# A GRU and attention layer: VectorE's order around the gates and the first norm, and the PSUM bank of one transpose

## Chip, cores and metric

One core of one Trainium2 chip. The metric is the device time of one execution in microseconds, less being better. The kernel before takes 58.65 us, the median of 3 runs (58.57 to 58.78).

## What is computed

Two graph layers over 512 nodes with 128 features, each with a residual and a layer norm without weights. The first aggregates over edges and applies a GRU cell, the second is graph attention with 4 heads:

```python
agg = jnp.einsum('ij,jh,ijh->ih', adj, node_features, T)
gi = agg @ w_ih.T + b_ih
gh = node_features @ w_hh.T + b_hh
r = sigmoid(ir + hr); z = sigmoid(iz + hz)
nn_ = tanh(in_ + r * hn)
L0 = (1.0 - z) * nn_ + z * node_features
x = _layernorm(x + L0)
...
h = jnp.einsum('ni,hid->hnd', x, W)
energy = leaky_relu(s_src[:, :, None] + s_dst[:, None, :], 0.2)
attention = softmax(where(adj > 0, energy, NEG_INF))
x = _layernorm(x + einsum('hij,hjd->hid', attention, h))
```

The adjacency matrix is sparse (512 by 512, few ones), the edge table has one row of 128 for each pair of nodes.

## The kernel before, in words

The kernel is written for the five engines by hand: each engine has its own program (`@block.tensor`, `@block.vector`, `@block.scalar`, `@block.gpsimd`, `@block.sync`), and the order of the calls in it is the order of the engine's queue. Engines meet through semaphores: `then_inc` at the producer, `wait_ge` at the consumer. Nothing is reordered. A branch on `flag` takes a sparse or a dense path; with this input it is the sparse one, and only its order of calls is spoken of here (the dense path has a loop over both groups that the diff adjusts too).

Nodes lie as 4 tiles of 128. Tiles 0 and 1 are group 0, tiles 2 and 3 are group 1; many steps run once for each group g. Edges lie in 10 chunks of 128, in the order `ORDER`; five belong to each group. The steps around the change, for a group:

- **products** (`product`, line 1156): for each chunk, VectorE multiplies gathered edge rows with gathered source rows. The source rows come from TensorE (`source_rows`, line 603) through a PSUM bank, from which ScalarE copies them (`keep_xr`, line 402). k counts chunks in the order of use, so products 5 to 9 are those of group 1.
- **aggregate** (line 749, TensorE), then ScalarE's copy `keep_agg` (line 482), then TensorE's gate matmuls (`gates`, line 640), ScalarE's three tanh for r, z and the candidate (`gates`, line 437), and between them VectorE's `gated` (line 1078: the candidate before its tanh) and `mixed` (line 1087: three instructions that end in yT, the transposed sum of residual and GRU output).
- **raw_x1** (line 653, TensorE) transposes yT into a PSUM tile `y_ps`. `project` (line 662, TensorE) multiplies yT with the attention weights.
- **moments** (line 1102, VectorE): two bn_stats and two bn_aggr on `y_ps`. The reciprocal deviation comes for group 0 from GpSimd by a power (line 361), for group 1 from ScalarE's square root (`deviation`, line 446) and VectorE's reciprocal (`invert`, line 1096).
- **keep_u, split_u** (lines 1116 and 1162, VectorE): the attention logits' node terms, in three bf16 parts. **scaled_h** (line 457, ScalarE): h. **split_h** (line 1170, VectorE): the middle and the low bf16 part of h, the high one being h's own upper half. TensorE gathers h for each edge in three passes (`gather_h`, line 805): the pass s = 1 needs the middle part (`s_hres`), the pass s = 2 the low part (`s_hlo`).
- **normalise** (line 1123, VectorE): x1 itself, two instructions that read `y_ps`. x1 is only needed for the residual at the end; SP copies it (line 309) once all four tiles are there (`s_x1`).
- GpSimd adds up h (`h_sum`, lines 362 to 368) as soon as ScalarE has written it.

`y_ps` is PSUM bank 3, all four tiles. TensorE may not write into a bank in which VectorE is reading, so the group-1 `raw_x1` waits until x1 of group 0 is done (lines 656 and 657). Bank 2 holds the candidate's input part `in_ps`, its first half for group 0, its second half for group 1, and later the transposed logits and the numerators of tiles 0 and 1.

TensorE's order in the stretch: aggregate(0), gates(0), the source rows of the last groups, raw_x1(0), project(0), aggregate(1), gates(1), high and middle gathers of group 0, edge_logits(0), raw_x1(1), project(1), 28 more gather matmuls of which the last 12 need the low part of h, edge_logits(1), and so on (lines 768 to 829).

Of the kernel before, what the change touches and what calls it, by code (L numbers as in the profile page):

```python
# [10 lines left out]
ALU = mybir.AluOpType  # L11
# [9 lines left out]
NC = 10  # L21
# [6 lines left out]
def build_gnn(nc, x, x_turned, adj, adj_first, adj_turned, edge_table, w_hh, w_ih, w_gat, w_gat_turned, columns, out):  # L28
# [10 lines left out]
    with ExitStack() as ctx:  # L39
# [142 lines left out]
        in_ps = tiles4[2]  # L182
        y_ps = tiles4[3]
        sel_bank = [bank[2], bank[3]]
# [347 lines left out]
        def _(pe):  # L532
# [120 lines left out]
            def raw_x1(g):  # L653
                pe.wait_ge(s_yT, g + 1)
                pe.wait_ge(s_wcc, 1)
                if g == 1:
                    pe.wait_ge(s_x1, 2)
                for t in range(2 * g, 2 * g + 2):
                    mm = nc.tensor.transpose(y_ps[:, t], yT[:, t], ident[:])  # L659
                mm.then_inc(s_yp, 1)  # L660
# [275 lines left out]
        def _(dve):  # L936
# [159 lines left out]
            def invert(k):  # L1096
# [3 lines left out]
                nc.vector.reciprocal(rstd[:, ts], spread[:, ts]).then_inc(s_rstd, 1)  # L1100

            def moments(g, link):
                dve.wait_ge(s_yp, g + 1)
                for t in range(2 * g, 2 * g + 2):
                    ins = nc.vector.bn_stats(st6[:, t, 0], y_ps[:, t])
                link(ins)
                for t in range(2 * g, 2 * g + 2):
                    ins = nc.vector.bn_aggr(mv[:, t], st6[:, t, 0:1])
                if g == 0:
                    link(ins)  # L1110
                    nc.vector.tensor_scalar(epsv[:, 0:2], mv[:, 0:2, 1], 4 * EPS, None, ALU.add).then_inc(s_var, 1)  # L1111
                else:
                    ins.then_inc(s_var, 1)
                    invert(1)

            def keep_u(g):
# [4 lines left out]
                                        rstd[:, ts].unsqueeze(2).broadcast_to([P, 2, 2 * NH]), ALU.mult).then_inc(s_u, 1)  # L1121

            def normalise(g):
                for t in range(2 * g, 2 * g + 2):
                    nc.vector.tensor_scalar(x1[:, t], y_ps[:, t], mv[:, t, 0:1], rstd[:, t:t + 1], ALU.subtract, ALU.mult)\
                        .then_inc(s_x1, 1)

# [26 lines left out]
            with dve.If(sparse == 1):  # L1154
# [14 lines left out]

                def split_h(g):  # L1170

                    ts = slice(2 * g, 2 * g + 2)
                    dve.wait_ge(s_h, g + 1)
                    nc.vector.tensor_tensor(h_parts[:, 1, ts], h_parts[:, 0, ts], h3[:, 0, ts], ALU.subtract).then_inc(s_hres, 1)
                    dve.wait_ge(s_hres, g + 1)
                    nc.vector.tensor_tensor(h_parts[:, 2, ts], h_parts[:, 1, ts], h3[:, 1, ts], ALU.subtract).then_inc(s_hlo, 1)
# [3 lines left out]
                gated(0)  # L1180
                product(5)
                product(6)
                mixed(0, link)
                product(7)
                product(8)
                product(9)
                moments(0, link)
                keep_u(0)
                split_u(0)
                split_h(0)  # L1190
                gated(1)
                normalise(0)
                mixed(1, link)
                moments(1, link)
                keep_u(1)
# [8 lines left out]
                nc.vector.tensor_copy(zs[:], shared.unsqueeze(2).broadcast_to([P, 2, 2, NH])).then_inc(s_zs, 1)  # L1204
                split_h(1)
                dve.wait_ge(s_new, 1)
# [49 lines left out]
            with dve.Else():  # L1256
# [14 lines left out]
                for g in range(2):  # L1271
                    gated(g)
                    mixed(g, link)
                    moments(g, link)
                    keep_u(g)
                    normalise(g)
                dve.wait_ge(s_u, 2)
# [78 lines left out]
```

## Time and profile before

| what | value |
|---|---|
| median of 3 runs | 58.65 us |
| profiled execution, its own time | 58.71 us |
| its span, first to last instruction | 57.0 us |
| TensorE busy | 43.2 us (76%), 550 matmuls |
| VectorE busy | 39.6 us (70%), 155 instructions |
| ScalarE busy | 24.9 us (44%), 60 instructions |
| GpSimd busy | 14.6 us (26%) |
| mean granted TensorE clock | 0.969 |

How to read it: busy time is the time in which an engine had an instruction in work, as a share of the span. A busy engine isn't on the critical chain for that reason alone; the chain of waits, followed back from the last instruction, tells which work ended last at each point. In a timeline a merged row gives the start of the first and the time from there to the end of the last of several equal instructions, and in square brackets the idle time of the engine before it and what ended that. Starts of neighbours on VectorE and ScalarE overlap the end before by up to 0.1 us.

### The profile page before, as it was taken

The numbers are of one execution on the slowest core, as the hardware profiler recorded it, in microseconds if no ns is written. First come the engines' busy times: TensorE is split into PE (matmuls) and PEld (weight loads), VectorE is DVE, ScalarE is ACT, GpSimd is POOL, SyncE is SP. The second block draws the span as 40 slices with busy tenths as digits, with TensorE's granted clock in tenths as the row PEclk, the third lists the DMA queues.
The fourth block names the chain that finished last, engine by engine and source line by source line (L and its number), as shares of the span: only waits on it lengthen the run. The fifth ranks groups of instructions, "written<-read, shape, count | busy, mean of one in ns | idle before, by whom it ended". The sixth has DMA issues, their size and how long they took to land.

```text
span 57.0 us, 1512 instructions
## 1 busy us (share of the span) xinstructions
PE 43.2 (76%) x550; PEld 35.4 (62%) x550; DVE 39.6 (70%) x155; ACT 24.9 (44%) x60; POOL 14.6 (26%) x29
## 2 busy tenths in 40 slices
PE   0599687958799999999998979789769899900000
PEld 0133366758589695688996668687759699900000
DVE  3986989999994084702299369963789479999600
ACT  1904636509997343023944085932940191000520
POOL 1940001756767777400000531000510000000000
PEclk9999999999999999999999999999999999999755
DMA  0699970012113131310000000000024200000033
GB/s 0 182 313 340 384 257 0 6 46 58 46 46 46 46 72 32 66 26 0 0 0 0 0 12 0 0 0 6 0 46 100 50 0 0 12 0 12 0 101 89
DMA packets 3033, 3.41 MB, mean 60 GB/s; under 512 B 560, under 2 KB 2096, under 8 KB 3024
## 3 DMA queue, kind: packets, MB, share of 16 engines
q1 hardware_dynamic: 2288, 2.49, 14.0%
q0 software_dynamic: 320, 0.66, 5.2%
q10 hardware_dynamic: 416, 0.14, 0.9%
q8 instruction: 6, 0.10, 0.7%
q14 instruction: 3, 0.02, 0.1%
HBM read 2.76 MB, written 0.26 MB: 53 GB/s over the span
## 4 chain that ended last, share of the span: by engine, by line
DVE 46%; PE 35%; ACT 7%; issue 6%; DVEq 0%; ACTq 0%
DVE colhot L1003 9%; PE bank L676 6%; PE bank L615 6%; PE bank L759 3%; PE bank L808 3%; PE bank L637 3%; DVE st L1136 2%; DVE x1n L1244 2%; DVE held L987 2%; DVE rowhot L992 2%; DVE zmax L1211 2%; DVE zmax_f L1208 2%; PE bank L659 2%; PE bank L763 2%; ACT out_sb L474 2%
## 5 line engine op out<-in xcount | busy, mean ns | idle before, releaser
L347 POOL DMA_INDIRECT edge<-in_L_gnn_edge_table,eidx x10 | 10.1, 1006 | 9.8 <-DVE eidx L1011 7.4
L615 PE MATMUL bank<-x_parts,colhot 128*128 128x128 bf16 x120 | 8.1, 218 | 0.0
L808 PE MATMUL bank<-h_parts,colhot 128*128 128x128 bf16 x120 | 7.9, 219 | 0.0
L615 PEld LDWEIGHTS bank<-x_parts,colhot 128*128 128x128 f16 x120 | 7.2, 96 | 0.3
L808 PEld LDWEIGHTS bank<-h_parts,colhot 128*128 128x128 f16 x120 | 7.3, 96 | 0.2
L1003 DVE TENSOR_TENSOR colhot<-bank,slot_mid 128x512 f16<-128x512 f32 x8 | 5.4, 684 | 0.2 <-PE bank L583 0.2
L676 PE MATMUL bank<-ones_adj 128*128 128x512 f16 x8 | 3.6, 631 | 2.0 <-DVE ones_adj L953 2.0
L405 ACT COPY xr<-bank 128x512 f32<-128x512 f32 (+1 forms) x6 | 3.3, 548 | 2.4 <-PE bank L624 2.4
L583 PE MATMUL bank<-rowhot,posm 128*128 128x128 f16 (+1 forms) x48 | 3.8, 213 | 0.7 <-DVE rowhot L992 0.4
L455 ACT ACT_TABLE_LOAD x3 | 3.8, 1283 | 0.1
L451 ACT ACTIVATE spread<-mv,eps_col 128x2 f32<-128x2 f32 (+1 forms) x2 | 0.6, 296 | 7.1 <-DVE mv L1141 5.7
L637 PE MATMUL bank<-xT,whhT 128*128 128x128 f32 (+1 forms) x12 | 3.7, 403 | 0.0
L1160 DVE TENSOR_TENSOR eprod<-edge,xr 128x128 f32<-128x128 f32 x10 | 2.4, 288 | 1.8 <-ACT xr L405 1.8
L583 PEld LDWEIGHTS bank<-rowhot,posm 128*128 128x128 f16 x48 | 2.9, 115 | 1.0 <-DVE posm L1028 0.6
L676 PEld LDWEIGHTS bank<-ones_adj 128*128 128x128 f16 x8 | 1.0, 141 | 3.7 <-DVE ones_adj L953 2.0
L593 PE MATMUL bank<-jcol,colhot 128*128 128x1 f16 x40 | 2.1, 164 | 1.4 <-DVE colhot L1003 0.7
L861 PE MATMUL bank<-vals,xr 128*128 128x132 f32 x24 | 2.9, 279 | 0.0
L396 ACT ACTIVATE posm<-bank,tot_in 128x512 f16<-128x512 f32 x3 | 2.1, 687 | 2.0 <-DVE tot_in L982 2.0
L593 PEld LDWEIGHTS bank<-jcol,colhot 128*128 128x128 f16 x40 | 1.7, 96 | 2.0 <-DVE colhot L1003 2.0
L361 POOL TENSOR_TENSOR rstd<-epsv,mhalf 128x2 f32<-128x2 f32 x1 | 0.7, 722 | 8.5 <-DVE epsv L1111 8.5
L484 ACT COPY aggT<-bank 128x256 f32<-128x256 f32 x2 | 0.7, 372 | 4.8 <-PE bank L763 4.8
L861 PEld LDWEIGHTS bank<-vals,xr 128*128 128x128 f32 x24 | 2.8, 190 | 0.0
(181 smaller groups left out, 98.1 us busy)
## 6 DMA issues: line engine op xcount, KB each, us to landing
adj_t<-in_adj_turned SPq DMA_DIRECT2D x3, 256.0 KB, 4.0
adj_i<-in_adj_first SPq DMA_DIRECT2D x1, 256.0 KB, 2.7
x_parts<-in_x SPq DMA_DIRECT2D x1, 256.0 KB, 3.6
xT<-in_x_turned SPq DMA_DIRECT2D x1, 256.0 KB, 4.4
x1n<-x SPq DMA_DIRECT2D x4, 64.0 KB, 2.7
whhT<-in_L_gnn_w_hh SPq DMA_DIRECT2D x1, 192.0 KB, 4.4
wT<-in_L_gnn_w_ih SPq DMA_DIRECT2D x1, 192.0 KB, 4.5
edge<-in_L_gnn_edge_table,eidx POOLq DMA_INDIRECT x10, 2.8
```

What stands on the lines that cost most here:

```text
L347: nc.gpsimd.indirect_dma_start(out=edge[:, c], out_offset=None, in_=edge_table, in_offset=bass.IndirectOffsetOnAxis(ap=eidx[:, c:c + 1], a ...
L405: nc.scalar.copy(xr[:, k].rearrange("p f h -> p (f h)")[:, 0:n], x_bank[k % 2][:, 0:n]).then_inc(s_xgc, 1)
L455: nc.scalar.activation(warm[:, k:k + 1], warm[:, 0:1], func)
L583: mm = nc.tensor.matmul(at, posm[:, t, jb::Q], src, start=True, stop=True)
L593: nc.tensor.matmul(idx_bank[:, c:c + 1], cols_at(jb, c), jcol[:, jb:jb + 1], start=(jb == 0), stop=False)
L615: nc.tensor.matmul(x_bank[k % 2][:, i * P:(i + 1) * P], cols_at(jb, c), x3[:, s, jb], start=(jb == 0 and s == 0), stop=(jb == Q - 1 and s ...
L637: return nc.tensor.matmul(at[:, cols], whhT[:, k], xT[:, ts.start:ts.stop].rearrange("h t p -> h (t p)"), start=(ts.start == 0), stop=(k = ...
L676: nc.tensor.matmul(bank[7], ones_adj[:, 0:P], ones_adj[:], start=True, stop=True)
L808: mm = nc.tensor.matmul(hg_at(c), cols_at(jb, c), h3[:, s, jb], start=(g == 0 and s == 0 and c % 4 == 0 and jb == 0), stop=False, skip_gro ...
L861: return nc.tensor.matmul(num_bank[t // 2][:, t % 2], rT_at(c, t), vals[:, c], start=False, stop=False, skip_group_check=True)
L1003: nc.vector.tensor_tensor(colhot[:, :, slots_of(c)], src.rearrange("p (j s) -> p j s", j=Q), want.unsqueeze(1).broadcast_to([P, Q, P]), AL ...
L1160: nc.vector.tensor_tensor(eprod[:, c], edge[:, c], xg_at(c), ALU.mult).then_inc(s_ep, 1)
```

## The change

In the sparse path's VectorE program, products 5 and 6, which stood between `gated(0)` and `mixed(0)`, now stand behind `mixed(0)` with the other three. `split_h` is cut into `middle_h` and `low_h`. `middle_h(0)` keeps its place ahead of `gated(1)`; `low_h(0)` stands between `mixed(1)` and `moments(1)`. `normalise(0)`, which stood between `gated(1)` and `mixed(1)`, is now inside `moments(1)`, behind the bn_aggr of group 1 and ahead of the reciprocal's wait for ScalarE. For group 1 `middle_h` and `low_h` follow each other as before. The tiles of `y_ps` for group 1 move to the first half of bank 2, and TensorE's wait for x1 of group 0 is gone. No instruction is added or taken out.

```diff
--- before.py
+++ after.py
@@ -180,7 +180,7 @@
         r_ps = tiles4[0]
         z_ps = tiles4[1]
         in_ps = tiles4[2]
-        y_ps = tiles4[3]
+        y_ps = [tiles4[3][:, 0], tiles4[3][:, 1], tiles4[2][:, 0], tiles4[2][:, 1]]
         sel_bank = [bank[2], bank[3]]
         x_bank = [bank[4], bank[5]]
         base_bank = bank[6][:, 0:3]
@@ -653,10 +653,8 @@
             def raw_x1(g):
                 pe.wait_ge(s_yT, g + 1)
                 pe.wait_ge(s_wcc, 1)
-                if g == 1:
-                    pe.wait_ge(s_x1, 2)
                 for t in range(2 * g, 2 * g + 2):
-                    mm = nc.tensor.transpose(y_ps[:, t], yT[:, t], ident[:])
+                    mm = nc.tensor.transpose(y_ps[t], yT[:, t], ident[:])
                 mm.then_inc(s_yp, 1)
 
             def project(g):
@@ -1099,10 +1097,15 @@
                 dve.wait_ge(s_std, k)
                 nc.vector.reciprocal(rstd[:, ts], spread[:, ts]).then_inc(s_rstd, 1)
 
+            def normalise(g):
+                for t in range(2 * g, 2 * g + 2):
+                    nc.vector.tensor_scalar(x1[:, t], y_ps[t], mv[:, t, 0:1], rstd[:, t:t + 1], ALU.subtract, ALU.mult)\
+                        .then_inc(s_x1, 1)
+
             def moments(g, link):
                 dve.wait_ge(s_yp, g + 1)
                 for t in range(2 * g, 2 * g + 2):
-                    ins = nc.vector.bn_stats(st6[:, t, 0], y_ps[:, t])
+                    ins = nc.vector.bn_stats(st6[:, t, 0], y_ps[t])
                 link(ins)
                 for t in range(2 * g, 2 * g + 2):
                     ins = nc.vector.bn_aggr(mv[:, t], st6[:, t, 0:1])
@@ -1111,6 +1114,7 @@
                     nc.vector.tensor_scalar(epsv[:, 0:2], mv[:, 0:2, 1], 4 * EPS, None, ALU.add).then_inc(s_var, 1)
                 else:
                     ins.then_inc(s_var, 1)
+                    normalise(0)
                     invert(1)
 
             def keep_u(g):
@@ -1119,11 +1123,6 @@
                 dve.wait_ge(s_rstd, g + 1)
                 nc.vector.tensor_tensor(u_sb[:, ts], proj_bank[g][:, :, H:H + 2 * NH],
                                         rstd[:, ts].unsqueeze(2).broadcast_to([P, 2, 2 * NH]), ALU.mult).then_inc(s_u, 1)
-
-            def normalise(g):
-                for t in range(2 * g, 2 * g + 2):
-                    nc.vector.tensor_scalar(x1[:, t], y_ps[:, t], mv[:, t, 0:1], rstd[:, t:t + 1], ALU.subtract, ALU.mult)\
-                        .then_inc(s_x1, 1)
 
             def residual(ts, ns):
                 return nc.vector.tensor_tensor(y2[:, ns].rearrange("p n (q d) -> p n q d", q=Q)[:, :, ts],
@@ -1167,30 +1166,31 @@
                     nc.vector.tensor_tensor(u_parts[:, ts, :, 2], u_parts[:, ts, :, 1], u3[:, ts, :, 1], ALU.subtract)\
                         .then_inc(s_u3, 1)
 
-                def split_h(g):
+                def middle_h(g):
 
                     ts = slice(2 * g, 2 * g + 2)
                     dve.wait_ge(s_h, g + 1)
                     nc.vector.tensor_tensor(h_parts[:, 1, ts], h_parts[:, 0, ts], h3[:, 0, ts], ALU.subtract).then_inc(s_hres, 1)
+
+                def low_h(g):
+
+                    ts = slice(2 * g, 2 * g + 2)
                     dve.wait_ge(s_hres, g + 1)
                     nc.vector.tensor_tensor(h_parts[:, 2, ts], h_parts[:, 1, ts], h3[:, 1, ts], ALU.subtract).then_inc(s_hlo, 1)
 
                 for k in range(5):
                     product(k)
                 gated(0)
-                product(5)
-                product(6)
                 mixed(0, link)
-                product(7)
-                product(8)
-                product(9)
+                for k in range(5, NC):
+                    product(k)
                 moments(0, link)
                 keep_u(0)
                 split_u(0)
-                split_h(0)
+                middle_h(0)
                 gated(1)
-                normalise(0)
                 mixed(1, link)
+                low_h(0)
                 moments(1, link)
                 keep_u(1)
                 split_u(1)
@@ -1202,7 +1202,8 @@
                                                     z_sb[:].rearrange("p c n -> p (c n)"), ALU.mult, ALU.max))
                 shared = z_all[:, 8 * NH:NC * NH].rearrange("p (g n) -> p g n", g=2)
                 nc.vector.tensor_copy(zs[:], shared.unsqueeze(2).broadcast_to([P, 2, 2, NH])).then_inc(s_zs, 1)
-                split_h(1)
+                middle_h(1)
+                low_h(1)
                 dve.wait_ge(s_new, 1)
                 dve.wait_ge(s_zT, 1)
                 nc.vector.tensor_tensor_scan(zmax_f[:], newrow[:, 0:VS], zT_bank[:, V0:V0 + VS], 0.0, ALU.add, ALU.max)\
@@ -1273,7 +1274,7 @@
                     mixed(g, link)
                     moments(g, link)
                     keep_u(g)
-                    normalise(g)
+                normalise(1)
                 dve.wait_ge(s_u, 2)
                 dve.wait_ge(s_v, 1)
                 with dve.Fori(0, Q) as t:
```

## Rows read from the trace of the kernel before

**Rows 1.** The page, part 4: the chain that ended last, by engine

```profile
DVE 46%; PE 35%; ACT 7%; issue 6%; DVEq 0%; ACTq 0%
```

**Rows 2.** Timeline of VectorE (start us, us, engine, line, operation, idle before)

```profile
28.55 0.49 DVE L1160 TENSOR_TENSOR eprod<-edge,xr 128x128 f32<-128x128 f32 x2 [1.05 <-ACT xr L405]
...
30.09 0.76 DVE L1160 TENSOR_TENSOR eprod<-edge,xr 128x128 f32<-128x128 f32 x3
...
34.06 0.56 DVE L1176 TENSOR_TENSOR h_parts<-h_parts 128x256 f32<-128x256 f32 x1
34.55 0.41 DVE L1082 SCALAR_TENSOR_TENSOR g_t<-g_r,hn_sb 128x256 f32<-128x256 f32 x1
...
35.33 0.72 DVE L1125 TENSOR_SCALAR x<-bank,mv,rstd 128x128 f32<-128x128 f32 x2
35.98 0.41 DVE L1091 SCALAR_TENSOR_TENSOR g_t<-g_z,xT 128x256 f32<-128x256 f32 x1
36.31 0.42 DVE L1093 SCALAR_TENSOR_TENSOR g_t<-g_z,g_n 128x256 f32<-128x256 f32 x1
36.76 0.42 DVE L1094 TENSOR_TENSOR yT<-g_t 128x256 f32<-128x256 f32 x1
37.71 0.50 DVE L1105 BATCH_NORM_STATS2 st<-bank 128x6 f32<-128x128 f32 x2 [0.53 <-PE bank L659]
38.25 0.25 DVE L1108 BATCH_NORM_AGGREGATE mv<-st 128x2 f32<-128x6 f32 x2
39.23 0.17 DVE L1100 RECIPROCAL rstd<-spread 128x2 f32<-128x2 f32 x1 [0.73 <-ACT spread L451]
...
42.10 0.42 DVE L1176 TENSOR_TENSOR h_parts<-h_parts 128x256 f32<-128x256 f32 x1
```

**Rows 3.** Timeline of ScalarE

```profile
30.04 0.48 ACT L405 COPY xr<-bank 128x384 f32<-128x384 f32 x1 [0.21 <-PE bank L624]
...
33.83 0.47 ACT L440 ACTIVATE g_r<-bank,bias_rz 128x256 f32<-128x256 f32 x1 [0.26 <-PE bank L645]
...
35.45 0.51 ACT L444 ACTIVATE g_n<-g_n,columns_sb 128x256 f32<-128x256 f32 x1 [0.28 <-DVE g_n L1084]
...
38.90 0.29 ACT L451 ACTIVATE spread<-mv,eps_col 128x2 f32<-128x2 f32 x1 [1.43 <-DVE mv L1108]
```

**Rows 4.** Timeline of TensorE's matmuls

```profile
30.23 0.44 PE L659 MATMUL bank<-ident,yT 128*128 128x128 f32 x2 [0.23 <-DVE yT L1094]
30.58 0.73 PE L665 MATMUL bank<-wcc,yT 128*128 128x136 f32 x4
...
36.48 0.19 PE L792 MATMUL bank<-u_parts,colhot 128*128 128x12 bf16 x2
37.24 0.44 PE L659 MATMUL bank<-ident,yT 128*128 128x128 f32 x2 [0.56 <-DVE yT L1094]
...
37.98 1.78 PE L808 MATMUL bank<-h_parts,colhot 128*128 128x128 bf16 x28
40.17 0.41 PE L792 MATMUL bank<-u_parts,colhot 128*128 128x12 bf16 x10 [0.41 <-DVE u_parts L1167]
```

**Rows 5.** Timeline of GpSimd

```profile
33.65 0.70 POOL L364 TENSOR_TENSOR h_sum<-h_parts 128x128 f32<-128x128 f32 x1 [1.09 <-ACT h_parts L463]
40.48 0.98 POOL L368 TENSOR_TENSOR h_sum<-h_sum,h_parts 128x128 f32<-128x128 f32 x2 [6.13 <-ACT h_parts L463]
```

**Rows 6.** Instructions of line 1125 (ns min/median/max, first and last start)

```profile
L1125 DVE TENSOR_SCALAR x<-bank,mv,rstd x4: 401/402/405, 35.3 to 40.3; 128x128 f32<-128x128 f32 x4
```

**Rows 7.** The chain that ended last, in order of time (start, us, what)

```profile
38.54 0.36 issue
...
52.79 0.05 issue
```

**Rows 8.** Stretches (busy us of PE, PEld, DVE, ACT, POOL; clock, DMA)

```profile
36.00:38.00 2.00, 1.44 (x34) 1.33 (x32) 1.43 (x6) 1.46 (x2) 0.00 (x0) 1.00 0.00 0
...
52.00:57.00 5.00, 0.00 (x0) 0.00 (x0) 1.57 (x11) 1.18 (x3) 0.00 (x0) 0.64 0.19 54
```

## The prediction

> **What bounds the kernel now.** I read the page first for the shares, then the chain of waits for what ends last, then the timelines of VectorE, ScalarE and TensorE over the stretch that the change touches, to see what each instruction on the chain really waited for. The chain gives VectorE 46% of the span and TensorE 35% [rows 1]: no engine is the bound throughout, and a saving counts only where it lies on the chain. So the question is which of the moved instructions lie on it.
>
> In the stretch from 28 to 40 us the chain is the one of the two GRU gates and the first norm. The VectorE timeline shows the group-1 part packed without a gap: middle and low parts of h of group 0, gated(1), normalise(0), mixed(1) [rows 2]. ScalarE's group-1 tanh of r ends at 33.83 + 0.47 = 34.30, but gated(1) starts at 34.55: it stood behind the low part of h (34.06 to 34.62). ScalarE's tanh of the candidate ends at 35.45 + 0.51 = 35.96, but its reader, the second instruction of mixed(1), starts at 36.31: it stood behind normalise(0) and the first of mixed(1) [rows 2, 3]. TensorE then idles 0.56 us before it transposes yT of group 1 at 37.24 [rows 4]. These are the two places where VectorE's order costs something.
>
> **Part A, group 0: products 5 and 6 behind mixed(0).** Before, mixed(0) stands behind two products that wait for ScalarE's copy until 28.55 [rows 2]. Without them its second instruction waits only for the tanh of the candidate, and yT of group 0 comes earlier by about the time of that wait, 1.05 us, and a little more. That is worth almost nothing, since other things hold the same place.
> - raw_x1(0) stands in TensorE's queue behind the source rows of the last x group and can start somewhat earlier than its 30.23 [rows 4]. But project(0) behind it waits for the last xr copy, which ends at 30.04 + 0.48 = 30.52 [rows 3] whatever VectorE does, since TensorE's own matmuls release it. So project(0) starts at about 30.56 in place of 30.58 [rows 4]: 0.02 us.
> - Products 7 to 9 now start one by one as their copies come; the last one waits for the same 30.52. Before, three products from 30.09 took 0.76, to 30.85 [rows 2]. At some 0.28 for one, the last ends at 30.82: 0.03 us for moments(0).
> - Products 5 and 6 (0.49 us together) fall behind yT, into time in which VectorE waits for the copy that product 7 reads: hidden. Without that wait they would cost 0.49 us before moments(0).
> Part A: 0.02 us gained. If the cover failed (a late product 9) it would cost what that product is late, up to one product, 0.28 us.
>
> **Part B, the low part of h of group 0 moved from before gated(1) to behind mixed(1).** gated(1) then starts when tanh of r is there, 34.30 less the 0.02 of part A, plus 0.02 for the signal, so about 34.32 at the latest instead of 34.55: 0.23 us. The low part costs 0.42 us where nothing disturbs it (42.10) and 0.56 here [rows 2]. In its new place it starts at about 36.55 and ends at 36.98, while TensorE transposes group 1; bn_stats(1), which took 0.47 from the start of the transposes (37.24 to 37.71) [rows 2, 4], is due at about 37.15. So it is covered with 0.17 us to spare; if yT came that much earlier still, it would be exposed by the rest. Its reader, the third pass of gather_h(0), stands behind raw_x1(1), project(1) and 16 of the 28 matmuls that follow from 37.98 [rows 4], so after about 38 us even in the new time, a full microsecond later than 36.98: nothing.
>
> Beside the low part runs GpSimd's h_sum, 33.65 to 34.35 [rows 5]: 0.70 us, while its two later sisters took 0.98 together, and the low part is 0.14 longer than its 0.42. It ends at 34.62, 0.27 after h_sum's end. So h_sum may hold a VectorE instruction that comes beside it, and gated(1) now would: 34.33 is h_sum's end less part A. Between nothing and 0.03 us; I take 0.02.
> The Trainium skill (page "SBUF — State Buffer", section "SBUF: two separate sides") says that GpSimd and a VectorE instruction with two SBUF inputs share a port pair exclusively, each for its whole length, the later one waiting. By that rule the sum would be the full 0.03 lower, without it 0.02 higher than mine; the trace agrees with it.
>
> **Part C, normalise(0) moved behind the moments of group 1.** Two instructions, 0.72 us from first start to last end, 0.65 from start to the next one's start (35.33 to 35.98) [rows 2]. Without them the first instruction of mixed(1) runs in the shadow of ScalarE's tanh, and the second starts when the tanh is done: 35.98 on the old times, where it started at 36.31: 0.33 us. The rest of the 0.65 had been hidden behind the tanh.
> In its new place normalise(0) stands between bn_aggr and the reciprocal of group 1. From the end of bn_aggr (38.25 + 0.25 = 38.50) to the reciprocal at 39.23 VectorE idles 0.73 us, for ScalarE's square root [rows 2, 3]. normalise(0) takes 0.65 of that, or 0.57 where its start overlaps the end of bn_aggr as starts do here: covered, with 0.08 to 0.16 us to spare. If the two didn't overlap at all (0.40 us each by themselves [rows 6]) they would cost 0.07. So from 0.07 lost to nothing; I take nothing, as the pair on record was overlapped.
> What this cover hangs on: the root starts 0.39 us after bn_aggr, of which the chain calls 0.36 "issue", while the same root in the last norm has 0.05 there [rows 7]. I can't say what that 0.36 is. If it is still there, the sum stands. If it goes, the root is ready 0.31 us earlier, but normalise(0) then holds the reciprocal, so at most 0.15 us more is gained.
>
> **Part D, the other bank.** The wait of raw_x1(1) for x1 of group 0 was fulfilled at 36.05, before yT (36.76 + 0.42) [rows 2]. So removing it alone gives nothing; it makes part C possible. Group 1 goes to bank 2's first half, whose last reader, gated(0), is long done. No instruction is added. I charge nothing for either.
>
> **Queues.** TensorE: the gathers and logits of group 0 in front of raw_x1(1) end at about 36.48 + 0.19 = 36.67 [rows 4]; the new yT is written by about 36.63, so TensorE is free just in time. Starts overlap ends by some 0.1 us there, so I charge nothing. ScalarE: the square-root table load and the small activation behind it follow the candidate's tanh; ScalarE had been idle 1.43 us before the root [rows 3], and they come earlier with the tanh, by 0.2 us. SP and GpSimd get their semaphores from the same chain. The 28 matmuls from 37.98 end before the logits of group 1, which wait 0.41 us for u [rows 4]; both move together. Behind that nothing changes, so what is won at raw_x1(1) should reach the end.
>
> **Sum.** 0.02 + 0.23 + 0.33 = 0.58 us, less 0.02 for h_sum: 0.56. raw_x1(1) starts at 36.68 instead of 37.24, just the idle time that TensorE had there. The profiled execution took 58.71 us (span 57.0), so 58.15; the median of the runs is 0.06 below the profiled one, so 58.09.
>
> **Rivals.**
> 1. TensorE becomes the bound. Its block before raw_x1(1) ends as yT comes. If it ends 0.2 us later than I read (modelled ends, or the source-row and gather passes stay where they were), the gain is 0.56 - 0.2 = 0.36 and the time 58.3. For: a margin of zero. Against: in the trace each matmul starts before the listed end of the one before. Chance 0.15.
> 2. The unexplained 0.36 before the root goes. Gain 0.56 + 0.15 = 0.71: 57.94. For: the other root doesn't have it. Against: nothing in the change touches ScalarE's stream. Chance 0.12.
> 3. The gain is mostly given back at normalise(0): the root isn't ready because ScalarE starts late, or normalise(0) is exposed with bn_aggr, by 0.4 us or more. For: 0.08 us of slack only. Against: VectorE idles there now, and the full exposure of 0.65 needs the root to wait for it. Gain about 0.1: 58.55. The same size comes out if part B and C were not on the chain. Chance 0.07. That would be "no change".
> 4. Slower: TensorE's clock. It is granted 1.00 from 36 to 38 us although the engine is busy only 1.44 of 2.00 us, and averages 0.64 from 52 to 57, where it does nothing [rows 8]. The change puts a new pause between raw_x1(0) and project(0) (0.3 us) and takes one away before raw_x1(1). If the clock fell to its lower level, 1.2 GHz, for the 28 matmuls (1.78 us), they would take 1.78 more; less the 0.41 of slack, 1.37 is lost and 0.56 won: 58.65 + 0.81 = 59.46. It decides once more than 0.97 us of matmul time runs at the low level. Against: the pauses now are as long and leave 1.00. Chance 0.05; with other losses 0.06 for slower.
> My own forecast has 0.60.
>
> **Numbers.** Predicted 58.09. The forecast's own bounds: 0.07 (normalise exposed), 0.1 on reading starts, up to 0.15 better: 57.93 to 58.3. With rivals 1 and 2 the range is 57.88 to 58.42, leaving out rivals 3 and 4 and the ends. About 0.3%, 0.18 us, is what a measurement of this kernel can tell from no change, so faster means under 58.47: forecast, rivals 1 and 2 together 0.87; same 0.07; slower 0.06.
>
> **What would show it.** Right: gated(1) starts within 0.03 of tanh r's end or of h_sum's; mixed(1)'s second instruction follows the candidate's tanh; TensorE's idle time before the second pair of yT transposes falls from 0.56 to below 0.1; the reciprocal still waits for ScalarE; project(0) starts where it did. Wrong: the reciprocal released by VectorE itself, the transposes of group 1 held by TensorE's own queue, bn_stats(1) starting behind the low part of h, or a clock below 1.00 before 50 us.

## The result, and the profile after

The changed kernel took 58.16 us, the median of 6 runs (57.97 to 58.37); the kernel before took 58.62 in 6 (58.40 to 58.78). The ratio is 0.9918 with a 95% interval of 0.9889 to 0.9948, so 0.48 us faster (0.30 to 0.65; the two medians differ by 0.46). The forecast was 58.09 us, 0.56 faster. On the chips of the runs further down, executions of one kernel fall into a fast and a slow group (63.3 to 66.5 us for the kernel before), and whole-time ratios there use the fast group alone.

The profiled execution of the changed kernel took 57.97 us, 0.74 less than the one before. Only 0.50 of that lies in the stretch that is followed here, from `gated(0)` to the end of ScalarE's last activation; 0.10 lies ahead of it and the rest behind it, where the output is sent off. Head, busy times and chain by engine:

```profile
span 56.2 us, 1512 instructions
...
PE 43.1 (77%) x550; PEld 35.3 (63%) x550; DVE 39.8 (71%) x155; ACT 24.9 (44%) x60; POOL 14.6 (26%) x29
...
PE 42%; DVE 41%; ACT 6%; issue 5%; DVEq 0%; ACTq 0%
```

Busy time is nearly the same as before; the share of the chain that [rows 1] gave VectorE has gone down and TensorE's is up. Part of that rise comes from group 0: the chain now runs through TensorE's source rows up to the last copy, not through VectorE's product 6 and mixed(0).

Starts in this profile are 0.10 us earlier than in the profile of before already at the first tanh of r (26.02 in place of 26.12), where nothing was changed. So what follows is read from the start of VectorE's `gated(0)`: 26.62 before, 26.52 after.

VectorE (line numbers have moved by a few: L1159 is the product, L1080 and L1082 gated, L1089 to L1092 mixed, L1179 the low part, L1102 normalise, L1098 the reciprocal), against [rows 2]:

```profile
29.76 0.50 DVE L1159 TENSOR_TENSOR eprod<-edge,xr 128x128 f32<-128x128 f32 x2 [0.50 <-ACT xr L405]
30.45 0.29 DVE L1159 TENSOR_TENSOR eprod<-edge,xr 128x128 f32<-128x128 f32 x1 [0.19 <-ACT xr L405]
...
34.23 0.42 DVE L1080 SCALAR_TENSOR_TENSOR g_t<-g_r,hn_sb 128x256 f32<-128x256 f32 x1 [0.31 <-ACT g_r L440]
...
35.69 0.42 DVE L1091 SCALAR_TENSOR_TENSOR g_t<-g_z,g_n 128x256 f32<-128x256 f32 x1 [0.17 <-ACT g_n L444]
36.15 0.43 DVE L1092 TENSOR_TENSOR yT<-g_t 128x256 f32<-128x256 f32 x1
36.49 0.42 DVE L1179 TENSOR_TENSOR h_parts<-h_parts 128x256 f32<-128x256 f32 x1
37.10 0.50 DVE L1108 BATCH_NORM_STATS2 st<-bank 128x6 f32<-128x128 f32 x2 [0.20 <-PE bank L657]
37.63 0.25 DVE L1111 BATCH_NORM_AGGREGATE mv<-st 128x2 f32<-128x6 f32 x2
37.80 0.70 DVE L1102 TENSOR_SCALAR x<-bank,mv,rstd 128x128 f32<-128x128 f32 x2
38.62 0.17 DVE L1098 RECIPROCAL rstd<-spread 128x2 f32<-128x2 f32 x1
```

ScalarE, against [rows 3]:

```profile
29.94 0.48 ACT L405 COPY xr<-bank 128x384 f32<-128x384 f32 x1 [0.21 <-PE bank L624]
...
33.73 0.47 ACT L440 ACTIVATE g_r<-bank,bias_rz 128x256 f32<-128x256 f32 x1 [0.26 <-PE bank L645]
...
35.15 0.51 ACT L444 ACTIVATE g_n<-g_n,columns_sb 128x256 f32<-128x256 f32 x1
...
38.29 0.29 ACT L451 ACTIVATE spread<-mv,eps_col 128x2 f32<-128x2 f32 x1 [1.12 <-DVE mv L1111]
```

TensorE's matmuls, against [rows 4]:

```profile
30.47 0.73 PE L663 MATMUL bank<-wcc,yT 128*128 128x136 f32 x4 [0.34 <-ACT xr L405]
...
36.38 0.19 PE L790 MATMUL bank<-u_parts,colhot 128*128 128x12 bf16 x2
36.63 0.44 PE L657 MATMUL bank<-ident,yT 128*128 128x128 f32 x2
...
37.37 1.78 PE L806 MATMUL bank<-h_parts,colhot 128*128 128x128 bf16 x28
39.56 0.41 PE L790 MATMUL bank<-u_parts,colhot 128*128 128x12 bf16 x10 [0.41 <-DVE u_parts L1166]
```

GpSimd's first sum of h, against [rows 5], and then the "issue" before the two roots in the chain, against [rows 7]:

```profile
33.54 0.69 POOL L364 TENSOR_TENSOR h_sum<-h_parts 128x128 f32<-128x128 f32 x1 [1.10 <-ACT h_parts L463]
```

```profile
37.93 0.36 issue
...
52.19 0.04 issue
```

What is to be seen, from group 0 on. Product 9 and project(0) are each released by ScalarE's last copy (29.94 + 0.48 = 30.42). project(0) starts 3.95 after gated(0), where before it was 3.96, and bn_stats(0), behind product 9, at 4.14 in both. gated(1) follows tanh r by 0.03 (33.73 + 0.47 = 34.20). The second instruction of mixed(1) follows the candidate's tanh (35.15 + 0.51 = 35.66), VectorE idling 0.17 us for it. The transposes at 36.63 follow the end of yT (36.15 + 0.43 = 36.58) by 0.05 and the listed end of the last logits (36.38 + 0.19 = 36.57) by 0.06, where TensorE had idled 0.56. bn_stats(1) waits 0.20 us for TensorE, so the low part (36.49 to 36.91) is covered. normalise(0) fills 37.80 to 38.50, the root ends at 38.29 + 0.29 = 38.58 and the reciprocal starts at 38.62. So the reciprocal still waits for ScalarE, though the view no longer lists idle time before it. The root's 0.36 of "issue" is still there. From gated(0), the reciprocal is at 12.10 instead of 12.61, and ScalarE's last activation ends at 27.34 instead of 27.84: what is won there, 0.5 us, arrives at the end.

The clock, against [rows 8]:

```profile
36.00:38.00 2.00, 1.95 (x40) 1.83 (x37) 1.73 (x8) 1.16 (x2) 0.00 (x0) 1.00 0.00 0
```

It is 1.00 throughout the stretch of the change, with TensorE now busy 1.95 of 2.00 us.

### The profile page after: what moved, and what is told of

Its sections match the earlier page's. It is cut to its first block, busy times and chain, and to the rows that moved or that the text cites. A ratio compares the mean times of both kernels' runs of the same rounds, so it can differ in the third digit from the quotient of the medians.

```text
span 56.2 us, 1512 instructions
## 1 busy us (share of the span) xinstructions
PE 43.1 (77%) x550; PEld 35.3 (63%) x550; DVE 39.8 (71%) x155; ACT 24.9 (44%) x60; POOL 14.6 (26%) x29
## 4 chain that ended last, share of the span: by engine, by line
PE 42%; DVE 41%; ACT 6%; issue 5%; DVEq 0%; ACTq 0%
PE bank L615 11%; DVE colhot L1001 9%; PE bank L674 6%; PE bank L757 3%; PE bank L806 3%; PE bank L637 3%; DVE st L1135 2%; PE bank L645 2%; DVE x1n L1245 2%; DVE held L985 2%; DVE rowhot L990 2%; DVE zmax L1212 2%; DVE zmax_f L1209 2%; PE bank L761 2%; ACT out_sb L474 2%
## 5 line engine op out<-in xcount | busy, mean ns | idle before, releaser
L1159 DVE TENSOR_TENSOR eprod<-edge,xr 128x128 f32<-128x128 f32 x10 | 2.4, 287 | 1.5 <-ACT xr L405 1.5
L380 ACT ACTIVATE adj_turn<-adj_t 128x512 f16<-128x512 int32 x3 | 1.9, 626 | 2.4 <-DMA adj_t<-in_adj_turned 2.4
L1080 DVE SCALAR_TENSOR_TENSOR g_t<-g_r,hn_sb 128x256 f32<-128x256 f32 x2 | 0.9, 426 | 2.9 <-ACT g_r L440 2.9
```

What stands on the lines that cost most here:

```text
L1159: nc.vector.tensor_tensor(eprod[:, c], edge[:, c], xg_at(c), ALU.mult).then_inc(s_ep, 1)
```

## The experiments

All times below are from the start of gated(0) in the profile of each run, in us: the start of gated(1), the start of the second pair of yT transposes, the start of the group-1 reciprocal, and the end of ScalarE's last activation. The runs were made on three other chips (1 to 4, 5 to 8 and 9 to 12 each on one), on which the stretch ahead of gated(0) is 5 to 8 us longer. The kernel before was timed there but not profiled; its shortest executions took 63.3 to 64.0 us, so the longer stretch is not the work of the edits. That stretch is unchanged code, and it varies from execution to execution by more than the effects looked for, so whole times say little here. For runs 4 to 8 there are only one to four of them, and no ratio. Behind gated(0) the granted clock was 1.00 up to the last matmul in every profile below, and the same kernel repeats to 0.02 us, as run 9 shows. Run 4, which is the kernel before but for one bank, stands within 0.01 us of the first row. Each run has one profile.

| run | gated(1) | transposes | reciprocal | end |
|---|---|---|---|---|
| before | 7.93 | 10.62 | 12.61 | 27.84 |
| changed | 7.71 | 10.11 | 12.10 | 27.34 |
| 1 products only | 7.92 | 10.61 | 12.60 | 27.84 |
| 2 low part only | 7.71 | 10.41 | 12.40 | 27.64 |
| 3 normalise and bank only | 7.92 | 10.31 | 12.30 | 27.55 |
| 4 bank only | 7.92 | 10.61 | 12.61 | 27.85 |
| 5 root without its second wait | 7.71 | 10.11 | 11.90 | 27.13 |
| 6 h_sum late, on before | 7.78 | 10.47 | 12.46 | 28.00 |
| 7 normalise(0) twice | 7.70 | 10.10 | 12.52 | 27.75 |
| 8 aggregate(1) first | 7.32 | 9.96 | 11.95 | 27.18 |
| 9 changed, again | 7.71 | 10.10 | 12.09 | 27.32 |
| 10 h_sum in the gap | 7.32 | 9.71 | 11.70 | 26.94 |
| 11 both | 7.33 | 9.72 | 11.34 | 26.58 |
| 12 tanh r early | 6.68 | 9.31 | 10.90 | 26.14 |

### 1. The products alone

```diff
                 gated(0)
-                product(5)
-                product(6)
                 mixed(0, link)
-                product(7)
-                product(8)
-                product(9)
+                for k in range(5, NC):
+                    product(k)
```

> The kernel before with products 5 and 6 behind mixed(0) and nothing else. My theory (the last xr copy holds project(0) and product 9): 0.00 to 0.03 us faster, project(0) starts 0.03 after the end of ScalarE's last xr copy, the transposes of yT of group 0 start about 0.4 us earlier. Rival (the products were on the chain): 0.1 us or more faster, with bn_stats(0) that much earlier against the first tanh of r.

```profile
37.11 0.29 DVE L1160 TENSOR_TENSOR eprod<-edge,xr 128x128 f32<-128x128 f32 x1 [0.19 <-ACT xr L405]
37.32 0.49 DVE L1105 BATCH_NORM_STATS2 st<-bank 128x6 f32<-128x128 f32 x2
```

The transposes of group 0 start 0.39 us earlier (3.22 from gated(0), before 3.61), but VectorE waits 0.19 us for ScalarE ahead of product 9, project(0) stays at 3.95 and bn_stats(0) at 4.14. The reciprocal gains 0.01 and the end nothing. Whole times: ratio 1.0018 (0.9916 to 1.0120). The part was hidden, as forecast.

### 2. The low part alone

`split_h` is cut in two as in the change, and then:

```diff
-                split_h(0)
+                middle_h(0)
                 gated(1)
                 normalise(0)
                 mixed(1, link)
+                low_h(0)
```

> The kernel before with only the low part of h of group 0 moved behind mixed(1); normalise(0) stays between gated(1) and mixed(1). Theory: gated(1) starts with the end of tanh r, 0.23 us earlier, and VectorE stays packed up to yT, so the transposes of group 1 come 0.22 us earlier and so does the end; bn_stats(1) still waits for TensorE and not for the low part. Rival (the low part is exposed in its new place): less than 0.1 us faster, with no idle time before bn_stats(1).

```profile
39.75 0.42 DVE L1082 SCALAR_TENSOR_TENSOR g_t<-g_r,hn_sb 128x256 f32<-128x256 f32 x1 [0.31 <-ACT g_r L440]
...
41.52 0.41 DVE L1093 SCALAR_TENSOR_TENSOR g_t<-g_z,g_n 128x256 f32<-128x256 f32 x1
...
42.92 0.50 DVE L1105 BATCH_NORM_STATS2 st<-bank 128x6 f32<-128x128 f32 x2 [0.19 <-PE bank L659]
```

gated(1) is 0.22 earlier, bn_stats(1) still waits 0.19 us for TensorE, and the reciprocal is 0.21 and the end 0.20 earlier. Whole times: 0.9943 (0.9880 to 1.0005).

### 3. normalise(0) and the bank alone

The changed kernel with this put back:

```diff
                 gated(0)
-                mixed(0, link)
-                for k in range(5, NC):
-                    product(k)
+                product(5)
+                product(6)
+                mixed(0, link)
+                product(7)
+                product(8)
+                product(9)
...
                 middle_h(0)
+                low_h(0)
                 gated(1)
                 mixed(1, link)
-                low_h(0)
```

> The changed kernel with the products and the low part of h put back, so only normalise(0) is moved and the bank changed. Theory: mixed(1)'s second instruction starts 0.02 after the candidate's tanh, 0.33 us earlier against gated(1) than before, and the reciprocal is still released by ScalarE: 0.30 to 0.33 us faster. Rival (normalise(0) gives it back before the reciprocal): under 0.1 us faster, the reciprocal starting with the end of normalise(0), more than 0.1 us after the end of the square root.

```profile
42.89 0.41 DVE L1080 SCALAR_TENSOR_TENSOR g_t<-g_r,hn_sb 128x256 f32<-128x256 f32 x1
...
44.34 0.42 DVE L1091 SCALAR_TENSOR_TENSOR g_t<-g_z,g_n 128x256 f32<-128x256 f32 x1 [0.24 <-ACT g_n L444]
```

The second instruction of mixed(1) waits 0.24 us for the candidate's tanh, where before it stood behind other work. The reciprocal is 0.31 earlier, the end 0.29. Whole times: 1.0176 (0.9995 to 1.0357), from no change to 3.6% slower. This ratio compares unlike executions: all five of this run had a mean granted clock of 0.885 to 0.895, those of the kernel before that it is set against 0.906 to 0.974. In this profile the clock was low ahead of gated(0) (0.54 from 20 to 28 us) and 1.00 from 32 us on, so the ratio says nothing on the change. The single parts, 0.01 + 0.21 + 0.31 = 0.53, come near the 0.51 of the whole.

### 4. The bank alone

```diff
-        y_ps = tiles4[3]
+        y_ps = [tiles4[3][:, 0], tiles4[3][:, 1], tiles4[2][:, 0], tiles4[2][:, 1]]
...
-                if g == 1:
-                    pe.wait_ge(s_x1, 2)
```

Each `y_ps[:, t]` becomes `y_ps[t]` with it.

> The kernel before with group 1 transposed into bank 2 and TensorE's wait for x1 of group 0 gone, nothing moved. Theory: the wait was long fulfilled, so nothing: within 0.03 us in the trace, the transposes of group 1 released by yT. Rival (the wait or the shared bank cost TensorE a start): the transposes start sooner after yT's end than the 0.05 us of before, and the time is 0.1 us less.

Nothing moved by more than 0.01 us. The bank is only what lets normalise(0) go.

### 5. The 0.36 us before the root

```diff
             def deviation(k):
-                act.wait_ge(s_eps, 2)
+                if k == 2:
+                    act.wait_ge(s_eps, 2)
                 act.wait_ge(s_var, k + 1)
```

> The changed kernel in which ScalarE's root for group 1 waits for the variances only and no longer also for the constant (set at the start). My prediction left open what the 0.36 us before that root is. Theory 1 (the second wait costs it): the root starts 0.07 after bn_aggr instead of 0.39, and normalise(0) becomes what holds the reciprocal, which comes about 0.12 earlier. Theory 2 (it belongs to something else, such as ScalarE's pause or the table): it stays at 0.36 to 0.40 and the reciprocal at 0.73 after bn_aggr.

VectorE and ScalarE around the root:

```profile
46.14 0.25 DVE L1112 BATCH_NORM_AGGREGATE mv<-st 128x2 f32<-128x6 f32 x2
46.30 0.70 DVE L1103 TENSOR_SCALAR x<-bank,mv,rstd 128x128 f32<-128x128 f32 x2
46.92 0.16 DVE L1099 RECIPROCAL rstd<-spread 128x2 f32<-128x2 f32 x1
```

```profile
46.42 0.29 ACT L452 ACTIVATE spread<-mv,eps_col 128x2 f32<-128x2 f32 x1 [0.75 <-DVE mv L1112]
```

The root starts 0.03 us after bn_aggr's end (46.14 + 0.25), not 0.41, so the wait for the constant, which VectorE writes at 2.6 us, was what it paid for. Runs 11 and 12 have the same edit and repeat the 0.03. The reciprocal starts 0.20 earlier than in the changed kernel (0.12 had been expected). The root ends at 46.71, and what holds the reciprocal until 46.92 is normalise(0), listed until 47.00: theory 1. It also says that normalise(0) had 0.20 us to spare in the changed kernel, more than the 0.08 to 0.16 of the prediction. In the last norm of the changed kernel the same pair of waits shows only 0.04 (52.19 above), so it isn't the price of two waits everywhere; what makes the difference stays open.

### 6. h_sum late, on the kernel before

```diff
-                pool.wait_ge(s_h, 1)
+                pool.wait_ge(s_h, 2)
                 nc.gpsimd.tensor_tensor(h_sum[:], h_parts[:, 0, 0], h_parts[:, 0, 1], ALU.add)...
-                pool.wait_ge(s_h, 2)
                 for t in (2, 3):
```

> The kernel before with GpSimd's first sum of h held back until h of group 1 is written, so that nothing of GpSimd runs beside the split of h of group 0. Theory (h_sum holds the low part): the low part takes 0.42 instead of 0.56 and gated(1) starts 0.14 us earlier against the first tanh of r; everything behind it 0.14 earlier. Rival (0.56 belongs to the instruction in that place): still 0.56.

```profile
39.59 0.42 DVE L1175 TENSOR_TENSOR h_parts<-h_parts 128x256 f32<-128x256 f32 x1
39.93 0.42 DVE L1081 SCALAR_TENSOR_TENSOR g_t<-g_r,hn_sb 128x256 f32<-128x256 f32 x1
...
46.95 0.47 DVE L1203 COPY zs<-z_all 128x16 f32<-128x16 f32 x1
```

```profile
45.86 0.47 POOL L364 TENSOR_TENSOR h_sum<-h_parts 128x128 f32<-128x128 f32 x1 [7.78 <-ACT h_parts L462]
46.40 0.99 POOL L367 TENSOR_TENSOR h_sum<-h_sum,h_parts 128x128 f32<-128x128 f32 x2
```

The low part takes 0.42 and gated(1) starts 0.15 earlier: the 0.14 of excess in [rows 2] was h_sum. But the end is 0.16 later than before, where 0.14 earlier had been expected. The three sums now run from 45.86 to 47.39, and VectorE's copy zs at 46.95, on the chain, takes 0.47 in place of 0.17: it is held until h_sum is through, and the reciprocal's 0.15 is paid back twice. The first sum itself, away from the split of h, takes 0.47 in place of 0.70.

### 7. How much cover normalise(0) leaves

```diff
                     normalise(0)
+                    for t in range(2):
+                        nc.vector.tensor_scalar(g_t2[:, t], y_ps[t], mv[:, t, 0:1], rstd[:, t:t + 1], ALU.subtract, ALU.mult)
                     invert(1)
```

> The changed kernel with normalise(0) issued twice between bn_aggr of group 1 and the reciprocal (the second time into a tile that nobody reads any more). Theory: normalise(0) leaves 0.12 us of the wait for the root, so the second pair (0.65) is exposed by 0.53: the reciprocal starts 1.26 after bn_aggr's end instead of 0.73, released by VectorE itself. Rival (more of it is hidden): exposed by less than 0.4.

```profile
44.94 0.25 DVE L1111 BATCH_NORM_AGGREGATE mv<-st 128x2 f32<-128x6 f32 x2
45.10 0.70 DVE L1102 TENSOR_SCALAR x<-bank,mv,rstd 128x128 f32<-128x128 f32 x2
45.72 0.72 DVE L1119 TENSOR_SCALAR g_t<-bank,mv,rstd 128x128 f32<-128x128 f32 x2
46.35 0.15 DVE L1098 RECIPROCAL rstd<-spread 128x2 f32<-128x2 f32 x1
```

The pair starts 0.09 before bn_aggr's end and each pair takes 0.62 to 0.63 to the next start, so the reciprocal comes 1.16 after bn_aggr's end, 0.42 later than in the changed kernel. That is 0.11 less than the theory's 0.53 and not under the rival's 0.4: neither had it right. With 0.63 issued, 0.21 was hidden: the same spare time as in run 5.

### 8. aggregate(1) ahead of project(0)

The profile after showed TensorE idle ahead of project(0) and project(0) ahead of the aggregate that the gates of group 1 wait for. On the changed kernel:

```diff
                 raw_x1(0)
+                aggregate(1)
                 pe.wait_ge(s_xgc, len(XGROUP))
                 project(0)
-                aggregate(1)
```

> The changed kernel with TensorE's aggregate(1) ahead of the wait for the last xr copy and of project(0). The trace of the changed kernel has TensorE idle for 0.34 us before project(0), and project(0) takes 0.57 that the gates of group 1 wait for while keep_u(0) waits for GpSimd's power anyway. Theory: the copy of the aggregate comes about 1.0 us earlier against the first tanh of r; then ScalarE's order (h of group 0 ahead of the gates) holds tanh r of group 1, so gated(1) and the end come 0.3 to 0.35 us earlier than in the changed kernel. Rival (project(0) is late for keep_u(0), or product 9 holds the aggregate): under 0.1.

```profile
41.08 0.43 DVE L1173 TENSOR_TENSOR h_parts<-h_parts 128x256 f32<-128x256 f32 x1 [0.32 <-ACT h_parts L463]
41.44 0.66 DVE L1080 SCALAR_TENSOR_TENSOR g_t<-g_r,hn_sb 128x256 f32<-128x256 f32 x1
```

```profile
41.12 0.70 POOL L364 TENSOR_TENSOR h_sum<-h_parts 128x128 f32<-128x128 f32 x1 [1.08 <-ACT h_parts L463]
```

The copy of the aggregate came 1.03 us earlier and gated(1) 0.39. But the end is only 0.16 earlier, half of the 0.3 to 0.35 that was expected. gated(1) now falls beside h_sum, and its first instruction takes 0.66 in place of 0.42. It ends at 42.10, 0.28 after h_sum (41.12 + 0.70); the low part in the kernel before ended 0.27 after h_sum. This is the hold that part B had weighed at 0.00 to 0.03 us; where the two really meet it costs 0.24.

The Trainium skill (page "SBUF — State Buffer", section "SBUF: two separate sides") has these two engines share a port pair that one of them holds for its whole instruction. Here the middle part starts first and h_sum takes 0.70 in place of the 0.47 of run 6, then h_sum ends and gated(1) goes on: the trace agrees in both directions. It doesn't show the whole listed length as held: gated(1) is through 0.28 after h_sum, not 0.42.

### 9. The changed kernel again

> The changed kernel once more, on the chip of the other runs of this set, as their measure. From the start of gated(0) its reciprocal of group 1 should stand at 12.10 us and its last ScalarE instruction end at 27.34, as in the first profile, if the stretch behind gated(0) is the same on every chip. Rival: the stretch differs by more than 0.05 from run to run, and the comparisons of single profiles are worth less.

Within 0.02 us on another chip. Whole times there: 0.9853 (0.9770 to 0.9937) of the kernel before.

### 10. h_sum in VectorE's wait for the root

On run 8:

```diff
                 pool.wait_ge(s_h, 1)
+                pool.wait_ge(s_var, 2)
                 nc.gpsimd.tensor_tensor(h_sum[:], h_parts[:, 0, 0], h_parts[:, 0, 1], ALU.add)...
```

> As the run with aggregate(1) first, and GpSimd's first sum of h held back until the variances of group 1 are there, so that it runs while VectorE waits for the root. In that run gated(1)'s first instruction took 0.66 beside h_sum in place of 0.42. Theory (h_sum holds a VectorE instruction with two operands in SBUF): 0.42 again, and the reciprocal 0.24 earlier, at 11.71 from gated(0); the end at 26.9 to 27.0. Rival (the 0.66 comes from ScalarE or TensorE reading the same gates): 0.66 stays, 11.95.

```profile
40.99 0.42 DVE L1081 SCALAR_TENSOR_TENSOR g_t<-g_r,hn_sb 128x256 f32<-128x256 f32 x1
```

0.42 again, the reciprocal at 11.70 and the end at 26.94, 0.24 before run 8. What the 0.66 was is shown by taking h_sum away from it. In its new place h_sum takes 0.46, and normalise(0), which reads PSUM and runs beside it, takes 0.69, as without it: neither holds the other. Whole times: 0.9813 (0.9732 to 0.9894).

### 11. The root's wait gone and normalise(0) parted

On run 10, the edit of run 5 and:

```diff
                 split_u(0)
+                normalise(0, 0)
                 middle_h(0)
...
-                    normalise(0)
+                    normalise(0, 1)
                     invert(1)
```

The second argument is the one tile that is done.

> The run before this one, with the root's second wait gone and the first tile of normalise(0) moved into VectorE's wait for h of group 0, so that only one tile is left between bn_aggr and the reciprocal. Theory: the reciprocal follows the root at 0.35 to 0.38 after bn_aggr's end, at 11.36 from gated(0), and the end comes at 26.6, 0.7 us before that of the changed kernel. Rival (one tile of 0.40 still holds the reciprocal, or the tile moved forward delays the middle part of h): 11.5 or later.

The reciprocal is at 11.34, 0.36 after bn_aggr's end, and the end at 26.58. The tile in front of the middle part costs 0.01. The logits of group 1, for which TensorE had idled 0.41 us, now follow its 28 gather matmuls with no idle time listed: TensorE and VectorE arrive there together, and a still earlier reciprocal alone would win next to nothing. Whole times: 0.9855 (0.9748 to 0.9962). The two executions behind it took 62.83 us each, 0.3 more than the 62.54 to 62.58 of run 10, so whole times don't bear the gain out; it rests on the anchored 0.36 of one profile.

### 12. tanh r ahead of h

On run 11:

```diff
                 keep_agg(1)
+                gate_r(1)
                 scaled_h(0, h_parts[:, 0], s_h)
-                gates(1)
+                gates(1, early=True)
...
                 split_u(0)
-                normalise(0, 0)
-                middle_h(0)
                 gated(1)
+                middle_h(0)
                 mixed(1, link)
                 low_h(0)
+                normalise(0, 0)
```

`gate_r` is the first of the three activations of `gates`, `early` leaves it out there.

> The run before this one, with ScalarE's tanh of r of group 1 ahead of its h of group 0, VectorE's gated(1) ahead of the middle part of h, and the first tile of normalise(0) behind the low part. Theory: gated(1) starts at 6.7 from gated(0) instead of 7.3, and TensorE's gathers and logits of group 0, not yT, then hold the transposes of group 1, at about 9.2; the reciprocal at 10.9, the end at 26.1 to 26.3. Rival (h of group 0 comes later and TensorE's block with it, by more than the gates win): the transposes no earlier than 9.5 and the end within 0.2 of the run before.

ScalarE's tanh r and h of group 0, and TensorE's block up to the transposes:

```profile
39.83 0.47 ACT L441 ACTIVATE g_r<-bank,bias_rz 128x256 f32<-128x256 f32 x1 [0.79 <-PE bank L653]
40.20 0.62 ACT L470 ACTIVATE h_parts<-bank,rstd 128x128 f32<-128x128 f32 x2
```

```profile
40.88 1.60 PE L814 MATMUL bank<-h_parts,colhot 128*128 128x128 bf16 x24 [0.22 <-ACT h_parts L470]
...
42.91 0.19 PE L798 MATMUL bank<-u_parts,colhot 128*128 128x12 bf16 x2
42.97 0.42 PE L665 MATMUL bank<-ident,yT 128*128 128x128 f32 x2
```

VectorE's yT:

```profile
42.26 0.42 DVE L1100 TENSOR_TENSOR yT<-g_t 128x256 f32<-128x256 f32 x1
```

The transposes follow the logits with no gap, at 9.31, although yT was there at 42.68, 0.29 before them. TensorE's own block holds them now, and it starts when h of group 0 is there (40.20 + 0.62). The reciprocal is at 10.90 and the end at 26.14, 1.20 us before the changed kernel and 1.70 before the kernel before. Whole times: 0.9689 (0.9604 to 0.9773) of the kernel before, faster than that; on that chip the changed kernel had 0.9853 (0.9770 to 0.9937). The three executions behind it, 61.65 to 61.96 us, all lie below the three of the changed kernel there, 62.71 to 62.95.

## Why the prediction was right

- **Part A**, 0.02: run 1 has 0.01 at the reciprocal. The last xr copy holds project(0) and product 9, as argued; the earlier transposes of group 0 are worth nothing.
- **Part B**, 0.23, with 0.02 off for h_sum: 0.22 at gated(1) and 0.21 at the reciprocal (run 2). The low part is covered in its new place with 0.20 us, forecast 0.17. In the changed kernel itself h_sum ends at 34.23, just when gated(1) starts, so nothing was lost to it. There was no margin in it: with gated(1) 0.39 us earlier (run 8) the same pair cost 0.24. The 0.14 of excess that the low part had was h_sum's (run 6).
- **Part C**, 0.33: 0.31 (run 3). The spare time of normalise(0) was under-read, 0.20 (runs 5 and 7) against 0.08 to 0.16, because its start overlaps bn_aggr and its length to the next start is 0.62, not 0.65. This changed nothing in the sum.
- **Part D**, nothing: 0.00 (run 4).
- **Sum**: 0.56 forecast, 0.51 in the profile at the reciprocal, 0.50 at the end, 0.48 in the whole times with an interval of 0.30 to 0.65. The parts alone give 0.53. Of the 0.05 between forecast and profile, part A is 0.01, B 0.02 and C 0.02 too large, the 0.02 charged for h_sum was not spent, and 0.02 is what the parts together give less than one by one. That is the size of reading signals and starts off a timeline; no step failed. The whole times alone, with their interval, could not tell 0.56 from 0.35.
- **Rivals.** TensorE as the bound (1): the last logits were listed until 36.57 and the transposes started at 36.63, so it was near to being one; run 12 shows what that bound looks like. The 0.36 (2) stayed; run 5 shows that it could be had and that normalise(0) then becomes the limit, as argued, but for 0.20 at the reciprocal where the prediction had at most 0.15: the under-read spare time of part C again. TensorE's slack of 0.41 before the logits of group 1 is still 0.41. Give-back (3) and the clock (4) did not come: the clock was 1.00 in every stretch read up to 51 us.

The pause that rival 4 needed can be seen elsewhere, in unchanged code. Stretches of run 1 on its chip:

```profile
20.00:22.00 2.00, 1.08 (x17) 0.93 (x18) 0.92 (x4) 0.59 (x1) 0.37 (x1) 0.73 0.12 33
22.00:24.00 2.00, 2.00 (x15) 1.22 (x12) 0.54 (x3) 0.00 (x0) 1.53 (x2) 0.50 0.12 33
...
30.00:40.00 10.00, 9.19 (x101) 8.14 (x101) 5.24 (x21) 4.24 (x11) 0.72 (x1) 1.00 0.00 0
```

And from VectorE's timeline in the same run:

```profile
20.60 0.69 DVE L1003 TENSOR_TENSOR colhot<-bank,slot_mix 128x512 f16<-128x512 f32 x1 [2.24 <-remote]
```

There VectorE's and with it TensorE's work paused ahead of gated(0). VectorE stood for 2.24 us in a wait that the profile can only put down to another core or a queue that it doesn't know; in the first chip's profile of the kernel before the same instruction has no idle time before it. TensorE was busy 0.58 us from 16 to 18, 1.15 from 18 to 20 and 1.08 from 20 to 22, and the granted clock was 0.73 in the last of these stretches and 0.50, the 1.2 GHz level, from 22 to 24; from 30 us on it was 1.00 again. Why those waits come on these chips and not on the first was not tried.

## What to carry to other kernels

Follow the critical chain one instruction at a time and ask of each whether its own operand or its place in the queue released it; work that stands in front of a waiting instruction costs only the part that reaches past its operand's arrival, and it belongs in the next true wait. An order is also a choice of neighbours across engines: GpSimd's small sum cost 0.24 us beside one instruction of the chain (run 8) and nothing in a gap (run 10). Where whole times scatter, compare stretches from a common start inside the profile.

## What was not expected of the hardware

- A semaphore wait that had long been fulfilled, ahead of the one that matters, delayed ScalarE's root by 0.38 us (0.41 after bn_aggr with it, 0.03 without). At the last norm's root the same pair shows only 0.04 to 0.05 of "issue"; the reason is open.
- A 128x16 copy of VectorE went from 0.17 to 0.47 us beside GpSimd's sum (run 6) and ended 0.03 after it: the short instruction lost 0.30, no less than the 128x256 one of run 8 with its 0.24.
- Moving a GpSimd sum that is not itself on the chain made the stretch 0.16 us longer (run 6, against the kernel before) or 0.24 shorter (run 10, against run 8), by what it fell beside.
